# A float32 attention product rewritten as three fp32r products, with its operands split on ScalarE and VectorE

## The reference

```python
xn = _layernorm(x)
x = x + _L0_attn_ref(xn, ...) + _L0_ffn_ref(xn, ...)

# _L0_ffn_ref: q, k and v each come from a tree-routed feed-forward net (16 leaves), then
scale = 1.0 / np.sqrt(LATENT)                    # LATENT = 256
attn = jax.nn.softmax(jnp.einsum('bqd,bkd->bqk', q, k) * scale, axis=-1)
return jnp.einsum('bqk,bkd->bqd', attn, v)       # one head, 8 batches of 1024 tokens, width 256
```

## Time and profile before

| what | value |
|---|---|
| median of 3 runs | 4403.33 us (4395.32 to 4408.93) |
| the profiled execution | 4398.99 us, its span on the core 4397.2 us |
| busy over the span | PE 90%, DVE 71%, ACT 65%, POOL 30% |
| mean granted TensorE clock | 0.936 |
| `mix_stage`, from its first gather to the end | 3870 to 4397 us |
| one batch of `mix_stage` (start of `turn_prob(0)` in one batch to that in the next) | 61.35 us |

### The profile page before, as it was taken

How to read it: one execution, slowest core, us unless ns; L and a number is a source line. 1 busy time by engine, 2 the same in 40 slices (tenths; PEclk the granted TensorE clock), 3 DMA queues, 4 the chain that set the end, 5 groups by cost and what they waited for, 6 DMA issues and landing times. The chain is left out here.

```text
span 4397.2 us, 76116 instructions
## 1 busy us (share of the span) xinstructions
PE 3937.4 (90%) x23970; PEld 1611.4 (37%) x23970; DVE 3106.2 (71%) x5547; ACT 2852.8 (65%) x3429; POOL 1330.7 (30%) x1618
## 2 busy tenths in 40 slices
PE   4489999999999999999999999999999477779999
PEld 2123223232322332332223223232322144458888
DVE  3567997888789789878987997888796122234444
ACT  0007887888788788878887887888889444422221
POOL 4211421242142123313221421342141344464330
PEclk7669999999999999999999999999999787789999
DMA  9610211111111111111111111111110366543220
GB/s 317 240 58 28 66 35 50 35 54 45 35 56 62 40 40 54 40 45 40 64 53 32 64 35 50 35 54 52 45 56 24 122 194 200 180 132 96 92 82 20
DMA packets 224807, 332.04 MB, mean 76 GB/s; under 512 B 29297, under 2 KB 165236, under 8 KB 219780
## 3 DMA queue, kind: packets, MB, share of 16 engines
q1 hardware_dynamic: 205956, 276.47, 19.3%
q0 software_dynamic: 18432, 50.36, 3.5%
HBM read 169.34 MB, written 156.34 MB: 74 GB/s over the span
## 5 line engine op out<-in xcount | busy, mean ns | idle before, releaser
L1514 DVE TENSOR_REDUCE arena<-psum 128x1 f32<-128x512 f32 x4096 | 2596.9, 683 | 474.9 <-PE psum L1087 438.8
L1318 ACT ACTIVATE arena<-psum,arena 128x1024 f32<-128x1024 f32 x2048 | 2163.0, 1111 | 193.4 <-PE psum L1125 170.3
L1087 PE MATMUL psum<-arena 48*128 48x512 f16 x4096 | 1383.6, 394 | 80.3 <-DVE arena L1514 22.3
L1141 PE MATMUL psum<-arena 128*32 128x512 f32 x8200 | 1107.3, 612 | 1.4 <-ACT arena L1242 0.7
L1087 PEld LDWEIGHTS psum<-arena 48*128 48x128 f16 x4096 | 322.9, 93 | 1645.0 <-DVE arena L1514 1115.5
L1125 PE MATMUL psum<-arena 50*128 50x512 f16 x4096 | 876.4, 383 | 52.2 <-issue 29.6
L1380 POOL TENSOR_TENSOR arena<-arena 128x16 f32<-128x16 f32 x129 | 28.8, 223 | 1775.6 <-DVE arena L1524 1775.6
L566 DVE TENSOR_TENSOR leaf_arena<-psum,leaf_arena 128x256 f32<-128x256 f32 x240 | 90.7, 420 | 314.8 <-PE psum L510 314.8
L1073 PE MATMUL psum<-arena 128*128 128x256 f32 x1024 | 289.8, 408 | 11.0 <-DVE arena L1514 11.0
L747 ACT ACTIVATE mix_arena<-psum,mix_arena 128x1024 f32<-128x1024 f32 x64 | 71.4, 1115 | 321.9 <-DVE mix_arena L767 321.8
L1125 PEld LDWEIGHTS psum<-arena 50*128 50x128 f16 x4096 | 210.1, 94 | 168.6 <-ACT arena L1318 90.1
(11 more groups left out here) (165 smaller groups left out, 3202.4 us busy)
## 6 DMA issues: line engine op xcount, KB each, us to landing
arena<-scratch_split SPq DMA_DIRECT2D x768, 64.0 KB, 2.1
scratch_split<-arena SPq DMA_DIRECT2D x64, 512.0 KB, 3.2
scratch_sorted_x<-route_arena SPq DMA_DIRECT2D x60, 512.0 KB, 8.1
leaf_arena<-scratch_sorted_x SPq DMA_DIRECT2D x60, 512.0 KB, 4.8
scratch_sorted_y<-leaf_arena SPq DMA_DIRECT2D x60, 512.0 KB, 3.2
leaf_arena<-in_leafw SPq DMA_DIRECT2D x3, 5128.0 KB, 19.2
arena<-in_x SPq DMA_DIRECT2D x18, 512.0 KB, 4.3
scratch_sum<-arena SPq DMA_DIRECT2D x18, 512.0 KB, 3.0
```

The source lines that it names most:

```text
L1087: nc.tensor.matmul(aux_bank[bank], ring[at, slot, 0, m, qt * P:(qt + 1) * P], ring[at, slot, 1, m, c * CH:(c + 1) * CH], start=True, stop=True
L1141: last = nc.tensor.matmul(value_bank[32 * j:32 * j + 32, :], vaug[:, kt, 2 * (s % PER_BATCH) + j % 2, :], prob[:, step % 2, j, :], start=k ...
L1318: nc.scalar.activation(prob[:, step % 2, 2 * h:2 * h + 2, :], score[:, 2 * h:2 * h + 2, :], ACT.Exp, scale=exp_scale[:, s % 2, s // 2:s // ...
L1514: nc.vector.tensor_reduce(halfmax[:, odd, 2 * m + h, qt, c:c + 1], aux_bank[bank], AX.X, ALU.max).then_inc(bank_used[bank], 1)
```

## The change

`probT` and `v` get high and low float32r parts, and each of the 8 products of a tile becomes three (`split_matmul`), as in the scores.

- `probT` is now a `Split`. ScalarE copies each turned bank into `probT.hi` (`high_prob`), VectorE writes bank minus `hi` into `probT.lo`; before, VectorE alone copied the bank.
- `vs` is a new `Split`, single buffered. Once in a batch ScalarE copies `v` into `vs.hi` (`high_v`, two instructions of 128x1024) and VectorE writes `vs.lo` (`low_v`, two of 128x1024). Both read `v` from SBUF.
- ScalarE's order changes. `Exp` of tile t + 1 goes ahead of `high_prob(t)`, and at t = 0 `high_v` stands between them. On VectorE `low_v` stands behind `turned_prob(0)`, ahead of `row_max(2)`.
- PE's `values(0)` waits for `v_split`, and so do the gathers of `v` two batches on, which waited for the last `values` of their batch.

```diff
     qk = Split(nc, ctx, "qk", [2, KC, SEQ])
+    probT = Split(nc, ctx, "probT", [2, TT, P])
+    vs = Split(nc, ctx, "vs", [TT, DIM])
...
-    probT = ar.take(2, TT, P)
...
-                        last = ("qk", b - 2, 4 * f + 3) if f < 2 else ("value", b - 2, TT - 1)
-                        pool.wait_ge(v_full, v_at[last] + 1)
+                        if f < 2:
+                            pool.wait_ge(v_full, v_at["qk", b - 2, 4 * f + 3] + 1)
+                        else:
+                            pool.wait_ge(v_split, 2 * (b - 2) + 2)
...
                 if t == 0:
-                    pe.wait_ge(gathered[2][b % 2], 16 * TT * (b // 2 + 1))
+                    pe.wait_ge(v_split, 2 * b + 2)
                 bank = take_v(v_at["value", b, t])
                 for kt in range(TT):
-                    last = nc.tensor.matmul(bank[:, 0:DIM], probT[:, t % 2, kt, :], v[:, b % 2, kt, :],
-                                            start=kt == 0, stop=kt == TT - 1)
+                    last = split_matmul(nc, bank[:, 0:DIM], probT, np.s_[:, t % 2, kt, :], vs, np.s_[:, kt, :],
+                                        kt == 0, kt == TT - 1)
...
+            def high_prob(b, t):
+
+                for h in range(2):
+                    k = v_at["prob", b, 2 * t + h]
+                    act.wait_ge(v_full, k + 1)
+                    nc.scalar.activation(probT.hi[:, t % 2, 4 * h:4 * h + 4, :].rearrange("p a b -> p (a b)"), bank_v(k), ACT.Copy
+                                         ).then_inc(prob_hi, 1)
+
+            def high_v(b):
+
+                act.wait_ge(gathered[2][b % 2], 16 * TT * (b // 2 + 1))
+                if b > 0:
+                    act.wait_ge(v_full, v_at["value", b - 1, TT - 1] + 1)
+                for h in range(2):
+                    at = slice(TT // 2 * h, TT // 2 * (h + 1))
+                    nc.scalar.activation(vs.hi[:, at], v[:, b % 2, at], ACT.Copy).then_inc(v_hi, 1)
+
             for u in range(8):
                 high(0, u)
             for b in range(BATCH):
+                exponential(b, 0)
                 for t in range(TT):
...
+                    if t + 1 < TT:
+                        exponential(b, t + 1)
+                    if t == 0:
+                        high_v(b)
+                    high_prob(b, t)
...
             def turned_prob(b, t):
                 for h in range(2):
                     k = v_at["prob", b, 2 * t + h]
-                    dve.wait_ge(v_full, k + 1)
-                    nc.vector.tensor_copy(probT[:, t % 2, 4 * h:4 * h + 4, :].rearrange("p a b -> p (a b)"), bank_v(k)
-                                          ).then_inc(v_used, 1)
+                    dve.wait_ge(prob_hi, 2 * (b * TT + t) + h + 1)
+                    probT.set_lo(nc, np.s_[:, t % 2, 4 * h:4 * h + 4, :], bank_v(k).rearrange("p (a b) -> p a b", a=4)
+                                 ).then_inc(v_used, 1)
+
+            def low_v(b):
+
+                for h in range(2):
+                    dve.wait_ge(v_hi, 2 * b + h + 1)
+                    at = slice(TT // 2 * h, TT // 2 * (h + 1))
+                    vs.set_lo(nc, np.s_[:, at], v[:, b % 2, at]).then_inc(v_split, 1)
...
                     turned_prob(b, t)
+                    if t == 0:
+                        low_v(b)
                     if 0 < t < TT - 1:
                         value(b, t - 1)
```

More of the change, by code:

```diff
@@ L591, in mix_stage @@
     hi_ready, nbias_ready, dchain = sem("hi_ready"), sem("nbias_ready"), sem("dchain")
+    prob_hi, v_hi, v_split = sem("prob_hi"), sem("v_hi"), sem("v_split")
     def bank_a(k):
@@ L734, in high, with exponential @@
                                      ).then_inc(hi_ready, 1)
+            def exponential(b, t):
+                act.wait_ge(a_full, a_at(b, t) + 2)
+                act.wait_ge(nbias_ready, b * TT + t + 1)
+                n = b * TT + t
+                if n >= 2:
+                    act.wait_ge(v_used, v_at["prob", (n - 2) // TT, 2 * ((n - 2) % TT) + 1] + 1)
+                bk = a_at(b, t) % 4 * CH
+                nc.scalar.activation(prob[:, t % 2, :], ps[:, bk:bk + SEQ], ACT.Exp, scale=FFN_SCALE,
+                                     bias=nbias[:, t % 2], accum_out=rowsum[:, b % 2, t]).then_inc(a_used, 2)
+            def high_prob(b, t):
[11 more added lines that the diff above has]
+                    nc.scalar.activation(vs.hi[:, at], v[:, b % 2, at], ACT.Copy).then_inc(v_hi, 1)
             for u in range(8):
```

## The result

The changed kernel takes 4412.59 us in the median of 20 runs (4404.25 to 4421.90), the kernel before 4401.18 in 20 (4381.80 to 4414.28). The ratio is 1.0027, 95% interval 1.0017 to 1.0038: slower by 12 us, where 20 were forecast. The prediction had called anything under 0.3% (13 us) too small to tell from none; twenty executions of each kernel do tell these 12 us from none. The profiled execution has a span of 4418.7 us. 6.0 us of its excess over the span before lie ahead of the first `turn_prob(0)` (3910.85 before, 3916.86 after), in work that the change does not touch (the first gather of the stage is already 6.3 us later); from there to the end it is 486.3 us before and 501.9 after, +15.5.

A forecast was written before the change was run, and what follows sets the result against it. PE was taken to bound the kernel. Per batch, 4.35 us (stall and batch end) less 4.0 gained plus 2.3 for the slow clock made +2.7, +20 in all: 4423 us, range 4396 to 4450.

The forecast's parts named there:

- Bound by PE, steady tiles hidden: Steady tiles: PE bounds, the two-engine path of `probT` is hidden, and the period falls from 7.06 to 6.49 us.
- The pass price: Value products: 0.120 us per pass of 256 columns, 24 passes 2.88 us, a gain of 0.57 us a tile.
- The surcharge of 0.014 us: Value products: extra time over one column a cycle, taken as fixed for each matmul with its weights.
- rival 2: After the gap before `values(0)`: the clock holds, 0.4 us a batch, 4406 us; chance 0.13.
- Rivals 1 and 3: Value products: 1, pass cheaper at 0.110, 4413 us, chance 0.17; 3, pass dearer at 0.136, 4442 us, chance 0.15.
- The stall: Start of a batch: `values(0)` waits for the split of `v`, PE stands 4.21 us, some 1.2 less in the first.
- Rival 4: Start of a batch: the split of `v` is no stall, -3.9 us a batch, 4373 us; chance 0.10.
- The slow clock: Behind the gap before `values(0)`: PE's passes run at 1.2 GHz, costing 2.3 us a batch.
- The row of 3.88 us idle: Clock evidence elsewhere in the trace: after 3.88 us without work, some 6 us at 1.2 GHz.
- The end of a batch: `turn_prob(6)` to `values(6)`: VectorE's chain makes it 7.45 us, swallowing tile 5's gain and 0.14 more.
- The sum: All terms: +2.7 us a batch, 21 over eight, less some 1.2 in the first: +20 us.

The follow-up runs named there:

- f3_small: Changed kernel, but in batches 1 to 7 `high_v` and `low_v` treat only 8 of 256 columns of `v`; 4375.5 us, ratio 0.9960 to the kernel before.
- the runs with 9 products: Changed kernel with PE running 9 identity products while it waits for the split of `v`; ratios 0.9940 and 0.9917, on chips of 4580 and 4563 us.
- g0_changed: The changed kernel unaltered, on the chip where the kernel before takes 4580 us; 4549.1 us against 4579.7, ratio 0.9924.
- h3_early_swap: Changed kernel, `v` split one batch early (batch 0's quarters at tiles 4, 5), `high_prob(t)` ahead of `Exp` of t + 1; 4563.8 us, kernel before 4563.4.
- f2_swap: Changed kernel with `high_prob(t)` ahead of `Exp` of tile t + 1 on ScalarE; 4375.1 us, ratio 0.9959 to the kernel before.
- the fillers: Changed kernel with PE running identity products while it waits for the split of `v`: 17 products 4403.7 us, ratio 1.0025; 9 products ratios 0.9940 and 0.9917.
- g3_early_swap: Changed kernel, `v` split one batch early (batch 0's quarters at tiles 4, 5), `high_prob(t)` ahead of `Exp`, on the 4580 us chip; ratio 0.9996.
- f4_early: Changed kernel with `vs` double buffered and `v` split one batch early, on a chip of 4400 us; 4378.1 us, ratio 0.9963 to the kernel before.

## Why the prediction came out as it did

- **Bound by PE, steady tiles hidden.** Right. The period fell from 7.08 to 6.50 us; nothing of the longer path of `probT` shows in it.
- **The pass price.** 0.120 us, measured 0.120 (365 of 512 distances from hi·hi to hi·lo are 0.120, most others 0.117 to 0.119 or at half clock). The surcharge of 0.014 us that the form with 512 columns has stays with 256, so it does not grow with the columns. The Trainium skill ("TensorE: Matmul & The Clock Gate", Back-to-back issue gap) gives N/2.4 + 2.5 ns for an isolated matmul at full clock; by it the estimate is 109 ns for 256 columns and 0.83 us gained a tile. The trace shows 0.120 us and 0.58. (The prediction says that with this figure its forecast would be the second rival's; by its own sum it is the first's, 4411.) Rivals 1 and 3 fall.
- **The stall.** `values(0)` 4.21 us late by the forecast, 4.16 measured; 1.2 less in the first batch, as forecast. Rival 4 falls, and f3_small shows that it is the split of `v`.
- **The slow clock.** It comes behind every gap, as forecast; rival 2 falls. Its size was the term most in error: 2.3 us a batch forecast, 1.3 to 2.8 measured, 2.06 in the mean of batches 1 to 7, 1.5 in the first. The row of 3.88 us idle stands for only half of the batches; in the others the clock was back after 3.4 us, as behind the shorter gap there. That is 2.4 us of the difference. That the slow clock costs this time and not the gap itself is shown by the runs with 9 products: 10.72 us from `turn_prob(1)` to `turn_prob(2)` with PE busy for part of the gap, 11.96 to 13.47 without.
- **The end of a batch.** `values(6)` starts 7.32 us after `turn_prob(6)`, not 7.45: the gain of tile 5 is swallowed, but the further 0.14 is not lost. That is 1 us more.
- **The sum.** By these terms it was 20 us; the stage shows 15.5. The slow clock makes 2.4 of the difference and the end of a batch 1; the rest is the stall and the gain of a tile, each right to some hundredths, and the last batch, which has no next one behind it and changes by 1.2 only. These errors all have one sign and add up; the forecast does not rest on errors that cancel, and no term is off by more than 3 us over the eight batches. The median moved by 11.4 (11.9 by the ratio), 4 below the profiled stage; runs of one kernel scatter over 18 to 32 us here, and that part has no known cause.
- **Missing.** The prediction noted that the gathers of `v` start earlier and that nothing waits for them. On two of the chips the order of gathers matters more than all the rest: there the changed kernel, in which the gathers of `v` stand apart from those of q and k and rows of 24 become 16 and 8, is 0.8% faster than the one before (g0_changed, on one of them). The kernel before was not traced there, so that its rows of 24 cost what h3_early_swap's do is inferred.

## What to carry to other kernels

A cheaper product on the engine that bounds is only worth what its preparation leaves. Here seven tiles of a batch gain 4.0 us and one wait for a split operand takes 4.2 and the clock of the next microseconds with it; find where the preparing engines stand idle (here a batch early, or with the ready `probT` copy ahead of `Exp`), and the same change gives 0.4% instead of costing 0.3%. Price a form that is not in the trace as columns over clock plus the surcharge of its nearest relative. And compare chips before settling on a gain: the same two kernels can change places. An empty instruction queue beside idle engines is no proof that they wait for code: see first whether one of them starts again while it is still empty.

## What the runs showed of the hardware

- After gaps of 4.0 us PE stood at 1.2 GHz for 3.4 or 6.8 us, after the one of 2.77 us in the first batch for 3.4; after gaps of 1.57 us (f2_swap) and 1.68 us (the fillers) it stayed at 2.4 GHz.
- A `Copy` of 128x1024 from SBUF takes 1.047 us on ScalarE, a subtraction of that size from SBUF 1.218 on VectorE.
- An fp32r product with its own 128x128 weights takes 0.227 us for 512 columns and 0.120 for 256, between starts at 2.4 GHz.
- On two of the three chips of the experiments PE stood idle beside a row of 24 indirect gathers for 15 to 19 us a batch (g3_early_swap) and 22 to 23 us (h3_early_swap) behind the first batch; with rows of 8 the same kernel takes 4448.4 us in place of 4563.8 on the second of them. On the third chip rows of 24 do no harm (f4_early). What holds the engines, and what differs between the chips, the traces don't say.
